# One Trainium2 core, attention and a top-2 expert layer: expert tiles of 128 rows instead of 256, and the boundary between the two blocks rearranged

## The reference

```python
x = x + tanh(g_xattn) * attention(layernorm(x), ctx, ctx)   # causal, 16 heads, biases
h = layernorm(x)
logits = h @ Wr + br                                        # 8 experts
weights = softmax(where(logits >= second_largest, logits, -inf))
e = gelu(einsum("td,edh->eth", h, W1) + b1)                 # exact gelu
y = einsum("eth,ehd->etd", e, W2) + b2
x = x + tanh(g_ffn) * einsum("etd,te->td", y, weights)
```

## Time and profile before

| | |
|---|---|
| runs | 907.29, 907.57, 908.5 us (median 907.57) |
| the profiled execution's own time | 904.24 us |
| its span (first to last instruction) | 902.5 us |
| mean granted TensorE clock | 0.959 of 2.4 GHz |
| PE busy, DVE, ACT, POOL | 88%, 65%, 48%, 40% of the span |
| first block | 0 to 469 us |
| second block | 469 to 902.5 us |

### The profile page before, as it was taken

One profiled execution on the slowest core, in us unless ns is written; L12 is line 12 of the kernel. 1 busy time (PEld: TensorE's weight loads), 2 busy tenths in 40 slices (PEclk: granted clock), 3 DMA queues, 4 the chain that ended last, 5 costly groups with the idle time before them and its releaser, 6 DMA issues. The chain is left out here.

```text
span 902.5 us, 24791 instructions
## 1 busy us (share of the span) xinstructions
PE 797.3 (88%) x7316; PEld 722.0 (80%) x7317; DVE 586.5 (65%) x1453; ACT 432.2 (48%) x955; POOL 364.3 (40%) x397
## 2 busy tenths in 40 slices
PE   3399999999999999998319999999999999999990
PEld 3289888888898888898218888888888888888880
DVE  2268999999999999988706454555545455545440
ACT  2156556665565665665105444444444444444440
POOL 2134555555565565656400233232322333332232
PEclk9699999999999999999559999999999999999996
DMA  8776887777778899984449644434333334433222
GB/s 187 135 138 123 178 177 153 135 154 157 166 162 215 198 214 222 193 172 144 146 147 295 151 70 65 65 50 64 53 56 50 53 54 56 54 51 44 25 25 27
DMA packets 132876, 108.81 MB, mean 121 GB/s; under 512 B 67744, under 2 KB 126496, under 8 KB 130592
## 3 DMA queue, kind: packets, MB, share of 16 engines
q1 hardware_dynamic: 117376, 87.19, 45.1%
q0 software_dynamic: 14304, 19.15, 13.8%
q10 hardware_dynamic: 1088, 1.11, 0.4%
HBM read 36.60 MB, written 34.36 MB: 79 GB/s over the span
## 5 line engine op out<-in xcount | busy, mean ns | idle before, releaser
L1259 POOL DMA_INDIRECT out_rows<-yg,gates x78 | 126.6, 1623 | 317.6 <-issue 150.3
L1369 PE MATMUL bank<-xh,wts 128*128 128x256 f16 x1872 | 212.2, 274 | 24.2 <-issue 24.1
L1369 PEld LDWEIGHTS bank<-xh,wts 128*128 x1872 | 183.6, 98 | 46.9 <-issue 24.9
L1385 PE MATMUL bank<-wts,hh 128*128 x1872 | 210.6, 273 | 0.0
L1385 PEld LDWEIGHTS bank<-wts,hh 128*128 128x128 f16 x1872 | 183.2, 98 | 21.2
L1285 ACT ACTIVATE hf<-bank,b1t,gscale 128x256 f32<-128x256 f32 x312 | 154.8, 562 | 20.2 <-PE bank L1369 19.1
L532 POOL TENSOR_SCALAR_AFFINE_SELECT xh<-rowmax 128x512 bf16<-128x512 bf16 x128 | 94.3, 737 | 138.3 <-DVE rowmax L785 124.0
L1036 PE MATMUL bank<-va,probs 128*128 128x102 f32 x1024 | 138.9, 277 | 9.0 <-DVE ao L733 8.9
L1316 DVE TENSOR_SCALAR hh<-hf,hscale 128x512 f16<-128x512 f32 x156 | 77.9, 499 | 104.5 <-ACT hf L1285 102.2
L1036 PEld LDWEIGHTS bank<-va,probs 128*128 128x128 f32 x1024 | 125.5, 192 | 12.1 <-DVE ao L733 6.6
L1295 ACT ACTIVATE yg<-yb,gates 128x256 f32<-128x256 f32 x78 | 35.4, 501 | 199.7 <-DVE yb L1327 148.0
(11 more groups left out here) (168 smaller groups left out, 983.9 us busy)
## 6 DMA issues: line engine op xcount, KB each, us to landing
wts<-in_W SPq DMA_DIRECT2D x16, 1024.0 KB, 6.6
wts<-keys SPq DMA_DIRECT2D x96, 128.0 KB
wts<-queries SPq DMA_DIRECT2D x96, 128.0 KB
split_weights<-wts SPq DMA_DIRECT2D x8, 1024.0 KB, 5.2
wts<-split_weights SPq DMA_DIRECT2D x8, 1024.0 KB, 7.6
xin<-in_x SPq DMA_DIRECT2D x16, 256.0 KB, 2.8
cin<-in_ctx_in SPq DMA_DIRECT2D x16, 256.0 KB, 3.6
out_rows<-x SPq DMA_DIRECT2D x16, 256.0 KB
```

The source lines that it names most:

```text
L1259: pool.indirect_dma_start(out=out[:, :], out_offset=bass.IndirectOffsetOnAxis(ap=numbers, axis=0), in_=yg[m % 2][:, half, :], in_offset=No ...
L1369: last = pe.matmul(HB[c // 2][:, c % 2 * TILE:(c % 2 + 1) * TILE], wts[:, bass.ds(expert[1], 1), at:at + P], xh[(m + 1) % RING][:, xp, k, ...
L1385: last = pe.matmul(YB[b][:, half * D:(half + 1) * D], hh[b][:, hp, c, half * P:(half + 1) * P], wts[:, bass.ds(expert[0], 1), at:at + D], ...
```

## The change

- `TILE` is 128: 71 tiles. A layer 1 product has 128 moving columns, not 256; layer 2 of a tile is 24 products, not 48. Both layers' PSUM banks, `hf` and the waits go by halves of a tile's chunks instead of quarters, and `hf` has two buffers. There is one scatter-add for a tile.
- The rows of tiles 0 and 1 are no longer loaded in the first block. SP loads tiles 0 to 3 at the start of the second, and then tile i+4 in round i (`AHEAD`). What waits until the scattered rows have landed is now SP in the second block (`rows_landed`), not POOL in the first.
- The weights of experts 4 to 7 are read back one expert a round in rounds 0 to 3.
- ACT ends the first block with one Gelu of a 128x1 column.
- Behind the last group, the router's products have 8 columns, not 64.
- The padding of each expert is 128 rows, not 256, and part of the table's scratch lies elsewhere.

```diff
-TILE = 2 * P
+TILE = P
...
+AHEAD = 4
...
-                sp.wait_ge(params, 16 * 10)
-
-                sp.wait_ge(env["table_ready"], 1)
-                sp.wait_ge(env["pads_in"], 16 * E)
-                sp.wait_ge(env["rows_placed"], 1)
-                for j in range(2):
-                    load_rows(sp, env, env["tile_row"][0:1, j:j + 1], env["first_xh"][j], j)
+                sp.wait_ge(params, 16 * 9)
...
-                for i in range(2):
-                    for b in range(GT):
-                        arrived(pool, scattered[b], NG - 2 + i, i, 2)
                 with pool.If(ties > 2):
+                    rows_landed(pool, scattered)
...
-                pool.sem_inc(env["rows_placed"], 1)
...
+                act.activation(ex[:, 0, 0:1], lgs[:, 0, 0:1], ACT.Gelu)
...
+                                many = MANY if there(g) else 1
...
-                    if there(2) and not (isinstance(i, int) and i < 0):
-
-                        j = i + 2
-                        when(sp, before(j, RING), added[1], added_value(j - RING))
+                    if there(AHEAD):
+
+                        j, k = i + AHEAD, (m + AHEAD) % RING
+                        when(sp, before(j, RING), added, added_value(j - RING))
...
-                    if isinstance(i, int) and -1 <= i <= 1:
-
-                        for e in {-1: (EARLY,), 0: (EARLY + 1,), 1: range(EARLY + 2, E)}[i]:
-                            sp.wait_ge(weights_in, 16 * 2 * e)
-                            load_weights(sp, wts, w_dram, e, weights_in)
-
+                    if isinstance(i, int) and 0 <= i < E - EARLY:
+
+                        sp.wait_ge(weights_in, 16 * 2 * (EARLY + i))
+                        load_weights(sp, wts, w_dram, EARLY + i, weights_in)
+
+                sp.wait_ge(table_ready, 1)
+                sp.wait_ge(pads_in, 16 * E)
+                rows_landed(sp, scattered)
+                sp.wait_ge(rows_placed, 1)
...
                         for c in range(HC):
-
-                            when(pe, c % 2 == 0 and before(i + 1, 1), gelu_ready, i * 4 + c // 2 + 1)
+                            half = c // 4
+
+                            when(pe, c % 4 == 0 and before(i + 1, 2), gelu_ready, (i - 1) * 2 + half + 1)
                             for q, (wp, xp, k) in enumerate(terms):
                                 at = wp * 2048 + k * H + c * P
-                                last = pe.matmul(HB[c // 2][:, c % 2 * TILE:(c % 2 + 1) * TILE],
+                                last = pe.matmul(HB[2 * b + half][:, c % 4 * TILE:(c % 4 + 1) * TILE],
...
-                        for half in range(2):
-                            for q, (hp, wp, c) in enumerate(terms):
-                                if half == 0 and q % 6 == 0:
-                                    pe.wait_ge(split_ready, i * 4 + q // 6 + 1)
-                                at = 4096 + wp * 2048 + c * D
-                                last = pe.matmul(YB[b][:, half * D:(half + 1) * D],
-                                                 hh[b][:, hp, c, half * P:(half + 1) * P],
-                                                 wts[:, bass.ds(expert[0], 1), at:at + D], start=q == 0, stop=q == 23)
+                        for q, (hp, wp, c) in enumerate(terms):
+                            if q % 12 == 0:
+                                pe.wait_ge(split_ready, i * 2 + q // 12 + 1)
+                            at = 4096 + wp * 2048 + c * D
+                            last = pe.matmul(YB[b][:, 0:D], hh[b][:, hp, c, :],
+                                             wts[:, bass.ds(expert[0], 1), at:at + D], start=q == 0, stop=q == 23)
```

More of the change, by code:

```diff
@@ L70, in load_rows, with rows_landed @@
                          transpose=True).then_inc(env["row_in"][j], 16)
-    sp.dma_start(env["gates"][j][:, :, :], rows[:, D:].rearrange("(h p) r -> p h r", h=2)
-                 ).then_inc(env["row_in"][j], 16)
+    sp.dma_start(env["gates"][j][:, :], rows[:, D:]).then_inc(env["row_in"][j], 16)
+def rows_landed(eng, scattered):
+    for i in range(2):
+        for b in range(GT):
+            eng.wait_ge(scattered[b][i], (NG // 2) * 2 * 16)
 def load_weights(sp, wts, w_dram, e, done):
@@ L415, in it @@
                         load(out[T:T + P, :], padrow[:, 0:D])
-                        for half in range(2):
-                            at = E * REG + half * P
-                            load(xs_dram[at:at + P, :], padrow[:, :])
+                        load(xs_dram[E * REG:E * REG + TILE, :], padrow[:, :])
                     if there(g + 1):
@@ L1191, in pipeline @@
             first = -(-(lo + 1) // RING) * RING if hi > MAIN_TILES else hi
-            rounds = (hi - 3 - first) // RING if hi > MAIN_TILES else 0
-            peeled(lo - 2, first)
+            rounds = (hi - AHEAD - first) // RING if hi > MAIN_TILES else 0
+            peeled(lo - AHEAD, first)
             if rounds:
@@ L1251, in it @@
                     if there(0):
[L1253 to L1258, removed]
-                            pool.indirect_dma_start(
-                                out=out[:, :], out_offset=bass.IndirectOffsetOnAxis(ap=numbers, axis=0),
-                                in_=yg[m % 2][:, half, :], in_offset=None, compute_op=ALU.add
-                                ).then_inc(added[half], 16)
+                        pool.wait_ge(yg_ready, i + 1)
+                        when(pool, before(i, 1), added, added_value(i - 1))
+                        settled(pool)
+                        numbers = gates[m][:, E:E + 1].bitcast(I32)
+                        pool.indirect_dma_start(
+                            out=out[:, :], out_offset=bass.IndirectOffsetOnAxis(ap=numbers, axis=0),
+                            in_=yg[m % 2][:, :], in_offset=None, compute_op=ALU.add).then_inc(added, 16)
                 def last(tiles):
-                    for half in range(2):
-                        pool.wait_ge(added[half], added_value(tiles - 1))
+                    pool.wait_ge(added, added_value(tiles - 1))
+                pool.sem_inc(rows_placed, 1)
                 pipeline(pool, it, 0, MAIN_TILES)
@@ L1292, in it @@
                         act.wait_ge(yb_ready, i + 1)
-                        when(act, before(i, 2), added[1], added_value(i - 2))
-                        for half in range(2):
-                            act.activation(yg[m % 2][:, half, :], yb[m % 2][:, half, :], ACT.Copy,
-                                           scale=gates[m][:, half, bass.ds(e, 1)]).then_inc(yg_ready, 1)
+                        when(act, before(i, 2), added, added_value(i - 2))
+                        act.activation(yg[m % 2][:, :], yb[m % 2][:, :], ACT.Copy,
+                                       scale=gates[m][:, bass.ds(e, 1)]).then_inc(yg_ready, 1)
                 all_tiles(act, it)
@@ L1308, in it @@
                         b = (m + 1) % 2
-                        for quarter in range(4):
-                            c = slice(2 * quarter, 2 * quarter + 2)
-                            dve.wait_ge(gelu_ready, (i + 1) * 4 + quarter + 1)
-                            when(dve, quarter == 0 and before(i + 1, 2), y_psum, i)
+                        for half in range(2):
+                            c = slice(4 * half, 4 * half + 4)
+                            dve.wait_ge(gelu_ready, (i + 1) * 2 + half + 1)
+                            when(dve, half == 0 and before(i + 1, 2), y_psum, i)
                             high = hh[b][:, 0, c, :].rearrange("p c t -> p (c t)")
-                            full = hf[:, c, :].rearrange("p c t -> p (c t)")
+                            full = hf[b][:, c, :].rearrange("p c t -> p (c t)")
                             step(dve.tensor_scalar(high, full, hscale[:, bass.ds(e, 1)], None, ALU.mult))
@@ L1341, in _ @@
                         step(dve.tensor_scalar(tile_no[:, :], tile_no[:, :], float(MAIN_TILES), None, ALU.add))
-                        rows_of_tiles(dve, step, env, lo, min(lo + MAIN_TILES, ALL_TILES))
+                        rows_of_tiles(dve, step, table, lo, min(lo + MAIN_TILES, ALL_TILES))
                     dve.sem_inc(rest_ready, 1)
```

69 lines of the change are left out of this document (36 added, 33 removed).

## The result

The changed kernel takes **1050.88 us** (median of 4 runs, 1050.26 to 1054.09), the kernel before 908.04 us beside it on the same chip. The ratio is **1.160, 95% interval 1.157 to 1.163**: 16% slower.

What follows compares the result with a forecast made beforehand. TensorE's sequencer was taken to bound the tiles: start 466 + 4.3 (tile 0's layer 1) + 70 x 7.75 + 3.5 (last layer 2) + 11.3 (tail) = 1027.6 us span, +125, so 1033 on the median; range 1008 to 1062.

Steps and rivals of the forecast that it cites:

- The bound: In the tiles: TensorE's sequencer, not its arithmetic (5.4 us), sets the cadence at 7.75 us a tile; 80 in 100.
- The tile's price: Sequencer's time for one 128-row tile: reads 1.6, layer 1 4.3, layer 2 1.9, less 0.05 for waits: 7.75 us.
- The start: At the block boundary: TensorE starts near 466 us against 470.4, 4 us earlier, with bounds of 463 and 472.
- the four issues: SP's issues before tile 0: 5.06 us before, taken as 4.5 for half the rows.
- Dummy Gelu and router: End of first block: Gelu takes the table load off the first tile, no wait hung on it; narrow router products 0, at most -0.5.
- The tail: From TensorE's end to the kernel's end, one scatter left: 11.3 us instead of 21.3.
- TensorE's 5.4 us a tile: Rival in the tiles: register instructions speed up and TensorE stays the bound, 5.4 us a tile, median 876; 8 in 100.
- SP's 6.4: Rival in the tiles: sequencer fast, SP's load issues don't shrink, 6.4 us a tile, median 938; 3 in 100.
- the weight-load rival: Rival in the tiles: weight load plus 128-column product slower in long rows, 6.5 us a tile, median 946; 2 in 100.
- The clock: Rival in layer 1: granted clock falls to its 1.2 GHz level, 10.2 us a tile, median 1205; 5 in 100.
- Before, this is hidden: In the kernel before: the sequencer's work makes about 8.4 us of the 10.48 that TensorE computes for a tile.
- What would show it: Signs in the changed profile: layer 1 every 7.7 us, products 90 ns apart, 0.13 us steps, gaps at reads, clock 1.00.

Runs made afterwards that it cites:

- a_fixed: The changed kernel with every expert product taking expert 0's weights at a constant address, reads and waits kept: 980.46 us, ratio 1.084.

## Why the prediction was right, and 18 us short

*The bound.* Right. The sequencer set the cadence; without its register instructions a tile costs 6.95 us (a_fixed), and with half of SP's loads too 5.7: each bound showed when the one above it was removed.

*The tile's price.* This is the term that was mis-sized: "1.6 + 4.3 + 1.9 = 7.8 us; there are four waits fewer in it, for which I take off 0.05 us", so 7.75. It is 8.03: from 471.59 (layer 1 of tile 1) 70 tiles later 1031.00 + 2.9 = 1033.9. Of the 0.28 us, 0.2 lie in layer 2's part, 2.1 and not 1.9. The 16 register instructions take 1.9 from the first to the last and not 1.8 (the rows were rounded to 0.1), and 0.2 lie between the last and the read. The 0.05 taken off for the waits brought nothing that shows. 70 x 0.28 = 19.8 us, more than the whole error of 18 (the small ones cancel).

*The start.* Predicted 466, measured 464.4. POOL drained from 450.6 and not 453: it read `mostint` at 449.4, where I had put 451.5, and drained 1.2 us later.

```profile
L563 POOLq TENSOR_LOAD <-mostint x1: 722/722/722, 449.4 to 449.4; - x1
```

That time moves by some us from one execution to the next (448.1 and 454.0 above), so it is in part luck that the start came out within 2 us. But tile 0 to tile 1 took 7.2 us and not 4.3 (+2.9): rows of tile 1 that I had left out, because SP's price of a load doesn't shrink with the rows. I had put the four issues at 4.5, "anything from half of that to all"; it was all.

*Dummy Gelu and router.* The Gelu at nothing: nothing shows. The router was not run by itself.

*The tail.* Predicted 11.3 us from TensorE's end, measured 1049.2 - 1036.8 = 12.4: the last scatter had to wait for the one before.

*Sum:* start -1.6, tile 0 +2.9, tiles +19.8, last layer 2 -0.6, tail +1.1, together +21.6; the predicted span of 1027.6 becomes 1049.2. The prediction's 1033 stood 5.4 us above its span, the measured median only 1.7 above this one.

*The rivals.* TensorE's 5.4 us a tile was near (5.7 measured). SP's 6.4 was too low (6.95 measured): a kernel with SP as its bound took 980 us and not 938. The 6.5 us a tile of the weight-load rival didn't show: a pair takes 61 ns in rows of 48. The clock stayed at 1.00 in the tiles.

*A step that the sum didn't need, and that was read wrongly:* "Before, this is hidden: [...] about 8.4 us of the 10.48". As a sum it is true, but it isn't the room. The room at the reads is the lead of 2.1 us less a lump of 1.6, half a microsecond a tile.

*What would show it:* products 90 ns apart, 0.13 us steps, gaps at the reads and the clock came as written. One sign failed: SP was to wait for `added` in every round, and did in 34 of 62. It has 8.03 - 6.95 = 1.1 us a tile to spare, where the prediction gave it 7.75 - 6.4.

## What to carry to other kernels

Before making tiles smaller, add up what TensorE's sequencer does for each of them: a register instruction for a run-time address at 0.13 us with the product behind it, a read of a register at 0.65. It doesn't shrink with the tile, and no busy figure counts it. At the reads only the last 2 us of TensorE's work hid it here, so look at it part by part and not as a sum over the tile. Reads that must be there belong in the middle of a long row of products that need no new address: two extra ones cost nothing there. The changed kernel has no such row, and moving its own reads was not tried. Of a change with several parts, time the parts alone: here the boundary gained 5 us, and the tile took away 150 (1050.9 - 901.3).

## What the runs showed of the hardware

- TensorE's sequencer got at most about 2.1 us ahead of the engine, as long as 19 products of 109 ns with their weight loads take (2.1 in both kernels in which more reads made it show).
- A transposing load of 128 rows occupied SP for 1.14 us in the changed kernel, one of 256 rows for 1.15 in the kernel before (medians).
- With a run-time address for its weights, a row of 128-column products went at 90 ns each; with a constant address, 61 ns.
- With a gap of 2.1 us in every tile, TensorE's granted clock fell to 0.51 behind every second gap (mean 0.94 from 500 to 900 us); with a gap of 1.2 us in every tile it stood at 1.00.
- A full PE bar doesn't mean that TensorE is the bound: in the changed kernel layer 1 is one busy piece of 4.3 us, for 2.9 us of work.
